# Latent attention: scores made in both orientations, stacks loaded 16 channels at a time, GpSimd merging the diagonal

## The chip, the cores and the metric

The kernel runs on one core of one Trainium2 chip. The metric is the device time of one launch in microseconds (us). A core has a matrix engine (TensorE, PE in the profile, with PEld for its weight loads), a vector engine (VectorE, DVE), an activation engine (ScalarE, ACT), a general engine (GpSimd, POOL) and a queue that mostly issues DMAs (SyncE, SP). SBUF is the on-chip memory of 128 partitions; PSUM, also 128 partitions, has 8 banks of 512 f32 columns and takes what PE writes.

## The reference, cut to what matters

A two-layer decoder on x of shape 2 x 1024 x 256. The change touches only the first block, a latent attention with 16 heads of 16 channels, on the layer-normalised x:

```python
q, k, v = x @ Wq, x @ Wk, x @ Wv
latent_kv = (k + v) @ W_down_kv             # 64 wide
k_rec, v_rec = latent_kv @ W_up_k, latent_kv @ W_up_v
scores = clip(einsum('bhqd,bhkd->bhqk', qh, kh) / 16, -1e4, 1e4)
decay  = exp(-0.0001 * abs(i - j))          # i query, j key
scores = clip(scores * decay, -1e4, 1e4)
attn   = softmax(scores); out = (attn @ vh) @ Wo
```

After it come a cross attention over 77 context tokens, a quantised feed-forward, a linear attention, a second cross attention and a mixture of experts. None of these is changed.

## The kernel before, in words

The program is a row of blocks; within a block each engine runs its own list in order, and semaphores order the engines against each other. Where one block ends, all engines wait until the last is done, DMAs included. The blocks that matter here are `normalise` (leaves the normalised x turned in `k.xt`), `latent_projections`, `latent_attention` and `project_out`.

`latent_projections` (L302) walks 4 groups of 512 tokens. For each group PE makes four pieces of 128 channels by 512 tokens (two of q, two of k, L350 and L357), the latent (L339) and the values (L364). Each piece is split into three bf16 parts whose sum is the f32 value: ACT rounds (L422), DVE subtracts (L383) and takes the largest magnitude (L385), ACT rounds the rest (L429), DVE makes the third part (L390). SP stores the three parts to DRAM (L445), 384 KB a piece, 16 pieces.

`latent_attention` (L451) runs over 16 heads in a loop, two batches in its body, 8 query tiles of 128 each: 256 steps. Before each head and batch SP loads a stack of 96 rows for q and for k (six bands of 16 channels, which are the products of parts that are kept), 12 DMAs of 32 KB (L537, L541). A step, in the order of the engines:

- PE makes the scores of one query tile against 1024 keys, two matmuls of 512 columns (L578), into two PSUM banks. Two steps are in flight.
- DVE multiplies them with the decay and takes the row maximum in one instruction, out to SBUF (L659).
- POOL negates the maximum (L563), ACT takes the exponential of 1024 columns with it as bias and sums the row (L706).
- Three steps later PE turns the probabilities in eight 128 x 128 transposes (L588) into two banks, ACT copies three of four such banks back to SBUF (L521), DVE the fourth (L519).
- PE sums the values: `mix_part` (L603), each matmul with 32 weight columns, four side by side into the four quarters of a bank, 128 moving columns each. A short copy, a transpose and a scaling (L695, L612, L640) end four query tiles.

When POOL has negated the last maximum it clears a DRAM buffer of 5 MB used much later (`clear_slots`, L116). That DMA belongs to the block too.

The cross attention block (L733 on) is not changed, but it has instructions of the kinds the change uses: exponentials read straight from PSUM (L1019), a value sum with 512 moving columns in four column quarters (L871), and a maximum split in three bf16 parts on POOL (L930 to L936).

Of the kernel before, what the change touches and what calls it, by code (L numbers as in the profile page):

```python
# [21 lines left out]
P = 128  # L22
# [279 lines left out]
def latent_projections(k, v_heads, q_scratch, k_scratch):  # L302
# [5 lines left out]
    qk_ready, part1_done, rest1_done, part2_done, part3_done = (  # L308
        k.sem("qk_ready"), k.sem("part1_done"), k.sem("rest1_done"), k.sem("part2_done"), k.sem("part3_done"))
    v_ready, v_done = k.sem("v_ready"), k.sem("v_done")  # L310
    bound_own, largest_ready, largest_turned = k.sem("bound_own"), k.sem("largest_ready"), k.sem("largest_turned")
    stored = [k.sem(f"stored{s}") for s in range(4)]
    scale = 1.0 / 16.0
    NP = NG * 2 * KD
    with ExitStack() as c, nc.Block() as block:
# [3 lines left out]
        parts = k.sb(c, "parts", [P, 4, 3, G], BF16)  # L319
        rest = k.sb(c, "rest", [P, 4, G])  # L320
        largest = k.sb(c, "largest", [P, NP])
# [5 lines left out]
        def _(pe):  # L327
# [14 lines left out]

            latent(0)
            for g in range(NG):
                rows = slice(g * G, (g + 1) * G)
                for m in range(KD):
                    n = 4 * g + m
                    wait(pe, rest1_done, n - 3)
# [5 lines left out]
                for m in range(KD):  # L354
                    n = 4 * g + 2 + m
                    wait(pe, rest1_done, n - 3)
# [4 lines left out]
                for j in range(TPG):  # L361
                    t = g * TPG + j
                    wait(pe, v_done, t - 1)
                    pe.matmul(k.ps[:, 5 + t % 2, 0:D], lat[:, t * P:(t + 1) * P], k.wuv[:, :],  # L364
                              start=True, stop=True).then_inc(v_ready, 1)
# [6 lines left out]
        def _(dve):  # L372
# [4 lines left out]
            for g in range(NG):  # L377
                for n in range(4 * g, 4 * g + 4):
                    s = n % 4
                    dve.wait_ge(part1_done, n + 1)  # L380
                    wait(dve, part2_done, n - 3)
                    wait(dve, part3_done, n - 3)
                    dve.scalar_tensor_tensor(out=rest[:, s, :], in0=k.ps[:, s, :], scalar=scale if s < 2 else 1.0,  # L383
                                             in1=parts[:, s, 0, :], op0=ALU.mult, op1=ALU.subtract).then_inc(rest1_done, 1)
                    own.did(dve.tensor_reduce(largest[:, n:n + 1], parts[:, s, 0, :], AX, ALU.max, apply_absolute_value=True))  # L385
                for n in range(4 * g, 4 * g + 4):
                    s = n % 4
                    dve.wait_ge(part2_done, n + 1)
                    dve.wait_ge(rest1_done, n + 1)
                    dve.tensor_tensor(parts[:, s, 2, :], rest[:, s, :], parts[:, s, 1, :],  # L390
                                      ALU.subtract).then_inc(part3_done, 1)


            own.wait()
            by_piece = largest[:, :].rearrange("p (g a m) -> p g a m", a=2, m=KD)
            for side in range(2):
                ins = dve.tensor_reduce(sides[:, side:side + 1], by_piece[:, :, side, :], mybir.AxisListType.XY, ALU.max)
                if side == 0:
                    own.did(ins)
                    own.wait()  # L400
            ins.then_inc(largest_ready, 1)
# [5 lines left out]
            own.did(dve.tensor_scalar(k.inside[:, :], bound[:, :], 0.9 * CLAMP / HD, None, ALU.is_lt))  # L407
            own.wait()

        @block.scalar  # L410
        def _(act):
# [3 lines left out]

            copy_latent(0)
            for g in range(NG):
                for n in range(4 * g, 4 * g + 4):
                    s = n % 4
                    act.wait_ge(qk_ready, n + 1)  # L420
                    wait(act, stored[s], 16 * g)
# [29 lines left out]
def latent_attention(k, v_heads, attn, decay, q_scratch, k_scratch):  # L451

    nc = k.nc
    k.next_block()
# [1709 lines left out]
```

## Time and profile before

| what | us |
|---|---|
| median of 3 runs | 1612.59 (1612.44 to 1614.67) |
| the profiled execution's own time | 1615.76 |
| its span in the trace | 1614.2 |
| latent projections, from their first work to the next block's | about 22.7 to 84.0 |
| latent attention, to the first work of the output projection | 84.0 to 622.2 |

PE is busy 83% of the span, DVE 57%, ACT 58%, POOL 12%. A row of groups gives line, engine and operation, names, shapes and count, then busy time and the mean duration of one, then idle time before. A timeline row gives start, length, engine, line, names and count. Instructions on one engine overlap at their ends, so the distance of two starts, not the length of one, is what an instruction costs in a stream.

### The profile page before, as it was taken

To read this page: it belongs to the slowest core of one execution; us is meant where nothing else is said; L and a number is where in the kernel's file an instruction comes from. 1 tells how busy PE (TensorE), PEld (TensorE's weight loads), DVE (VectorE), ACT (ScalarE), POOL (GpSimd) and SP (SyncE) were. 2 spreads that over 40 slices of the span, in tenths; PEclk is the share of its full clock that TensorE was granted. 3 is DMA by queue.
4 is the path that set the end of the run, shared out by engine and by line. 5 is a ranking of instruction groups with operands and counts; after the bars stand their busy time and mean duration, and the time that the engine had idled before them with its cause. 6 is when DMAs were issued, how large, how long until landed. Compare 5 with 4: busy or idle time off the path is not lost. (4 is left out here: it accounts for less than half of the span.)

```text
span 1614.2 us, 36474 instructions
## 1 busy us (share of the span) xinstructions
PE 1340.0 (83%) x12288; PEld 960.2 (59%) x12291; DVE 919.8 (57%) x2059; ACT 930.1 (58%) x1793; POOL 190.5 (12%) x546
## 2 busy tenths in 40 slices
PE   5879999999999995898365699889874489999992
PEld 2347777777777774544223464364354279999992
DVE  5558888888888873532788844563354223323233
ACT  2469999999999991355375377624631033333330
POOL 0001111111111110111200000031120701111110
PEclk9879999999999997899756899988995589999996
DMA  3311010010101013200000100033006211111115
GB/s 115 131 51 31 22 27 24 24 26 23 29 20 29 20 38 110 80 1 4 16 1 0 31 1 1 1 120 129 1 4 212 102 34 36 37 36 38 36 33 166
DMA packets 60025, 74.30 MB, mean 46 GB/s; under 512 B 13006, under 2 KB 47728, under 8 KB 59952
## 3 DMA queue, kind: packets, MB, share of 16 engines
q1 hardware_dynamic: 53168, 56.76, 11.9%
q0 software_dynamic: 4672, 14.50, 2.7%
q10 hardware_dynamic: 2112, 2.10, 0.4%
q8 instruction: 43, 0.70, 0.2%
q14 instruction: 30, 0.25, 0.0%
HBM read 50.43 MB, written 22.88 MB: 45 GB/s over the span
## 5 line engine op out<-in xcount | busy, mean ns | idle before, releaser
L659 DVE CUSTOM_DVE_ANT_0 probs_sb<-banks,decay_sb 128x1024 f32<-128x1024 f32 x256 | 308.2, 1221 | 43.6 <-PE banks L578 22.5
L706 ACT ACTIVATE probs_sb<-probs_sb,shift_sb 128x1024 f32<-128x1024 f32 x256 | 294.8, 1151 | 18.1 <-POOL shift_sb L563 16.4
L588 PEld LDWEIGHTS banks<-ident_sb,probs_sb 128*128 128x128 f32 x2048 | 238.3, 141 | 55.1 <-issue 22.9
L588 PE MATMUL banks<-ident_sb,probs_sb 128*128 128x128 f32 x2048 | 267.8, 274 | 0.9 <-ACT probs_t_sb L521 0.8
L521 ACT ACTIVATE probs_t_sb<-banks 128x512 f32<-128x512 f32 x384 | 214.7, 597 | 4.1 <-PE banks L588 2.3
L578 PE MATMUL banks<-k_stack_sb,q_stack_sb 96*128 96x512 bf16 x512 | 156.9, 389 | 14.0 <-DMA k_stack_sb<-k_parts 10.7
L603 PE MATMUL banks<-probs_t_sb,v_head_sb 128*32 128x128 f32 x4096 | 151.2, 277 | 0.7 <-ACT probs_t_sb L521 0.7
L1846 PEld LDWEIGHTS banks<-slots_xt_sb,tile_w_sb 128*128 128x128 f32 x1248 | 146.5, 193 | 1.9
L1846 PE MATMUL banks<-slots_xt_sb,tile_w_sb 128*128 128x128 f32 x1248 | 146.6, 276 | 0.0
L1858 PE MATMUL banks<-experts_w_sb,xt_sb 128*128 x624 | 141.2, 379 | 1.3 <-issue 1.3
L1892 ACT ACTIVATE slots_xt_sb<-banks 128x256 f32<-128x256 f32 x39 | 14.9, 383 | 213.8 <-PE banks L1832 213.8
L1858 PEld LDWEIGHTS banks<-experts_w_sb,xt_sb 128*128 128x128 f32 x624 | 115.5, 190 | 15.8 <-issue 1.7
L519 DVE COPY probs_t_sb<-banks 128x512 f32<-128x512 f32 x128 | 88.6, 692 | 57.7 <-PE banks L588 56.0
L603 PEld LDWEIGHTS banks<-probs_t_sb,v_head_sb 128*32 128x32 f32 x4096 | 100.3, 109 | 32.3 <-issue 31.4
L563 POOL TENSOR_TENSOR shift_sb<-peak_sb,minus_sb 128x1 f32<-128x1 f32 x256 | 48.5, 190 | 452.8 <-DVE peak_sb L659 452.8
L977 DVE TENSOR_REDUCE peak_sb<-banks 128x8 f32<-128x616 f32 x64 | 49.9, 798 | 87.8 <-PE banks L826 87.8
L1019 ACT ACTIVATE pt_sb<-banks,keyfill_sb 77x1024 f32<-77x1024 f32 x64 | 67.5, 1104 | 38.0 <-PE banks L857 37.1
L1902 ACT ACTIVATE xt_sb<-banks,tile_b_sb 128x128 f32<-128x128 f32 x312 | 84.7, 387 | 5.1 <-PE banks L1846 3.4
L1942 DVE COPY tile_w_sb<-experts_w_sb 128x2048 f32 x39 | 47.8, 1227 | 60.2 <-issue 28.0
L1927 DVE TENSOR_TENSOR is_best_sb<-slots_x_sb,tile_owned_sb 128x1 f32<-128x1 f32 x39 | 6.2, 159 | 122.2 <-DMA outputs_y<-slots_y_sb,output_row_sb 122.2
L253 POOL TENSOR_TENSOR x_sb<-x_sb,bb_sb 128x256 f32<-128x256 f32 x48 | 33.0, 732 | 337.2 <-DMA bb_sb<-in_L_attn_bo 276.7
L1881 POOL DMA_INDIRECT outputs_y<-slots_y_sb,output_row_sb x39 | 37.4, 959 | 258.7 <-DVE slots_y_sb L1955 154.0
(289 smaller groups left out, 1910.0 us busy)
## 6 DMA issues: line engine op xcount, KB each, us to landing
experts_w_sb<-in_L_ffn_W SPq DMA_DIRECT2D x16, 1024.0 KB, 11.9
q_stack_sb<-q_parts SPq DMA_DIRECT2D x192, 32.0 KB, 1.7
k_stack_sb<-k_parts SPq DMA_DIRECT2D x192, 32.0 KB, 1.8
slots_x<-zeros_sb POOLq DMA_DIRECT2D x1, 5031.0 KB, 22.6
slots_x_sb<-slots_x SPq DMA_DIRECT2D x39, 129.0 KB, 2.1
xt_sb<-outputs_y SPq DMA_DIRECT2D x8, 512.0 KB, 5.5
q_parts<-parts_sb SPq DMA_DIRECT2D x8, 384.0 KB, 3.0
k_parts<-parts_sb SPq DMA_DIRECT2D x8, 384.0 KB, 4.2
```

The source lines that it names most:

```text
L519: ins = eng.tensor_copy(dst, k.ps[:, 4 + half, :])
L521: ins = eng.activation(dst, k.ps[:, 4 + half, :], ACT.Copy)
L578: last = pe.matmul(k.ps[:, 2 * (s % 2) + half, :], qs[:, u, q * P:(q + 1) * P], ks[:, u, half * 512:(half + 1) * 512], start=True, stop=True)
L588: last = pe.transpose(k.ps[:, 4 + half, j * P:(j + 1) * P], pr[:, s % 4, (half * TPG + j) * P:(half * TPG + j + 1) * P], k.ident[:, :])
L603: last = pe.matmul(k.ps[32 * j:32 * j + 32, 6, 0:P], vh[:, u, kt, :], pt[:, j, gs % 2, kt, :], start=kt == 0, stop=kt == QT - 1)
L659: dve.tensor_tensor_reduce(out=pr[:, s % 4, :], in0=scores, in1=decay[:, off:off + S], scale=1.0, scalar=-3.0e38, op0=ALU.mult, op1=ALU.ma ...
L706: act.activation(pr[:, s % 4, :], pr[:, s % 4, :], ACT.Exp, bias=shift[:, s % 8:s % 8 + 1], accum_out=sums[:, (s // TPG) % 4, s % 4:s % 4 ...
L977: dve.tensor_reduce(peak[:, t % TPG, 2 * half:2 * half + 2, :], k.ps[:, bank:bank + 2, 0:SLOTS * C].rearrange("p r (s n) -> p r s n", n=C) ...
L1019: act.activation(pt[:, n % 2, 2 * half:2 * half + 2, :], k.ps[0:C, 2 * half:2 * half + 2, :], ACT.Exp, bias=key_fill[:, b:b + 1]).then_inc ...
L1846: last = pe.matmul(k.ps[:, 2 * u + f // HALF, (f % HALF) * P:(f % HALF + 1) * P], w1[:, u, kd, f * P:(f + 1) * P], xst[:, u, kd, :], start ...
L1858: last = pe.matmul(k.ps[:, 6, s * D:(s + 1) * D], ht[:, s, f, :], r.w2[:, bass.ds(e, 1), f, :].rearrange("p a n -> p (a n)"), start=f == 0 ...
L1902: ins = act.activation(ht[:, s, f, :], k.ps[:, 2 * s + f // HALF, (f % HALF) * P:(f % HALF + 1) * P], ACT.Gelu_apprx_tanh, bias=b1[:, s, f ...
```

## The change

`latent_projections` now makes two versions of every piece. Version 0 is multiplied by exp(-0.0001 i) for q and exp(+0.0001 j) for k, version 1 by the inverse, with a sign. The product of a version's q and k is then the score with its decay already in it, on one side of the diagonal. DVE multiplies and takes the maximum in one instruction (from PSUM), ACT rounds twice, DVE subtracts once and the third part is made by POOL. There are 32 pieces instead of 16, six buffers instead of four, and 32 stores of 384 KB. Two fade rows and two tables of the decay's width are loaded at the start of this block instead of one table before it. When the first batch's pieces are stored, SP also loads the first stacks.

`latent_attention` is written out without a loop, in 16 groups of four heads by four query tiles (512 queries). The four heads of a channel lie behind one another in DRAM, so that a load of 16 channels brings four heads: 256 KB for k, 128 KB for q. Per group:

- 16 query-major score tiles as before (1024 columns each, cut in two or three matmuls where the version changes), which now serve the maximum alone (`highest`: the same DVE instruction, its output unused). They run 22 tiles ahead of what follows.
- POOL splits the 16 x 2 maxima in three bf16 parts, PE turns them, ACT copies them, and one DMA writes them as rows 96 to 98 of the q stack. The k stack has -1 in those rows, so the key-major product comes out with the maximum taken off.
- Eight key tiles (steps): four key-major score matmuls of 512 queries, one a head, each followed by one exponential of 512 columns from PSUM to SBUF, through a ring of three banks. No probability is turned and no bank copied.
- On a tile that crosses the diagonal, every second step, a fifth unit makes 128 queries of the four heads in the other version. POOL keeps the later half of one and the earlier half of the other (`affine_select` twice) and adds them.
- Two steps later PE sums the values: four matmuls of 512 columns, side by side. The row sum comes from a column of ones in the values.
- Every group: four transposes, a reciprocal and a scaling.

```diff
-            pe.wait_ge(exp_done, n + 1)                       # turn: 8 transposes a step
-                        last = pe.transpose(k.ps[:, 4 + half, j * P:(j + 1) * P], ...
+            def select(g, i):
+                ...
+                pool.wait_ge(exp_done, unit_index(g, i, HEADS - 1) + 1)
+                pool.affine_select(later, later, [[0, HEADS], [1, P]], ALU.is_ge, 0.0, base=0,
+                                   channel_multiplier=-1).then_inc(selected, 1)
+                earlier = probs_d[:, s // 2 % 2, :, :]
+                pool.wait_ge(exp_done, unit_index(g, i, HEADS) + 1)
+                pool.affine_select(earlier, earlier, [[0, HEADS], [-1, P]], ALU.is_gt, 0.0, base=0,
+                                   channel_multiplier=1).then_inc(selected, 1)
+                pool.wait_ge(selected, 2 * (s // 2 + 1))
+                pool.tensor_tensor(later, later, earlier, ALU.add).then_inc(merged, 1)
```

The order on PE, and what it waits for:

```diff
+            pe.wait_ge(constants, 2)
+            for tile in range(TILES + LEAD):              # 22
+                scores(tile)
+                if tile == TILES + 1:
+                    turn_peaks(0)
+            for g in range(GROUPS):                       # 16
+                for i in range(QT):                       # 8
+                    if g * QT + i >= 2:
+                        sum_values(g * QT + i - 2)        # waits merged on odd i
+                    for x in range(2):
+                        for h in range(2 * x, 2 * x + 2):
+                            key_scores(g, i, h)           # waits for the bank three units back
+                        if x == 1 and i == TURN_STEP and g + 1 < GROUPS:
+                            turn_peaks(g + 1)
+                        if tile_at(g, i, x) < GROUPS * TILES:
+                            scores(tile_at(g, i, x))
+                    if on_diagonal(i):
+                        diagonal_scores(g, i)
+                    if i == 3 and g > 0:
+                        turn_mix(g - 1)
```

What POOL does at the start of the block, before PE may begin:

```diff
+            own.did(pool.memset(vh[:, :, :, :, :], 0.0))                                        # 128 x 2048 f32
+            own.wait()
+            pool.memset(stacks.k[ROWS:ROWS + PARTS, :, :, :, :], -1.0).then_inc(constants, 1)   # 3 x 16384 bf16
+            pool.wait_ge(constants, 1)
+            pool.tensor_copy(ident_b[:, :], k.ident[:, :]).then_inc(constants, 1)
```

In `latent_projections`:

```diff
+            def apply_fade(e):
+                ...
+                wait(dve, part3_done, e - 3)
+                dve.tensor_tensor_reduce(out=rest[:, e % 4, :], in0=k.ps[:, n % 4, :], in1=fade[:, side, half * G:(half + 1) * G], ...
+        @block.gpsimd
+            for e in range(NV):                           # 32
+                pool.wait_ge(part2_done, e + 1)
+                pool.wait_ge(rest1_done, e + 1)
+                pool.tensor_tensor(parts[:, e % SLOTS, 2, :], rest[:, e % 4, :], parts[:, e % SLOTS, 1, :],
+                                   ALU.subtract).then_inc(part3_done, 1)
```

`clear_slots` still comes last on POOL, after the last `select`.

## Rows read from the trace of the kernel before

**Rows 1.** Busy time by stretch: PE, PEld, DVE, ACT, POOL, then PE clock, DMA share, GB/s.

```profile
22.70:84.00 61.30, 48.26 (x106) 20.25 (x106) 31.60 (x55) 25.43 (x53) 0.00 (x0) 0.81 0.31 103
100.00:580.00 480.00, 476.15 (x6316) 352.36 (x6315) 388.70 (x724) 468.25 (x905) 53.56 (x272) 1.00 0.10 25
...
700.00:710.00 10.00, 8.94 (x87) 4.03 (x85) 3.03 (x5) 5.86 (x7) 1.67 (x8) 1.00 0.00 1
```

**Rows 2.** Groups by line, whole span.

```profile
L659 DVE CUSTOM_DVE_ANT_0 probs_sb<-banks,decay_sb 128x1024 f32<-128x1024 f32 x256 | 308.2, 1221 | 43.6 <-PE banks L578 22.5 <-issue 13.7 <-PE banks L588 4.4
L706 ACT ACTIVATE probs_sb<-probs_sb,shift_sb 128x1024 f32<-128x1024 f32 x256 | 294.8, 1151 | 18.1 <-POOL shift_sb L563 16.4
...
L521 ACT ACTIVATE probs_t_sb<-banks 128x512 f32<-128x512 f32 x384 | 214.7, 597 | 4.1 <-PE banks L588 2.3
```

**Rows 3.** Timeline, a steady step of latent attention: PE's three kinds of work, ACT's copies.

```profile
301.34 0.65 PE L603 MATMUL banks<-probs_t_sb,v_head_sb 128*32 128x128 f32 x16
...
301.92 0.60 PE L578 MATMUL banks<-k_stack_sb,q_stack_sb 96*128 96x512 bf16 x2
...
302.36 1.04 PE L588 MATMUL banks<-ident_sb,probs_sb 128*128 128x128 f32 x8
...
303.00 1.09 ACT L521 ACTIVATE probs_t_sb<-banks 128x512 f32<-128x512 f32 x2
```

**Rows 4.** Timeline, the cross attention: value sum with 512 columns, exponentials from PSUM.

```profile
702.55 0.38 PE L857 MATMUL banks<-peakt_sb,minus_one_sb 12*77 12x512 bf16 x2
702.78 2.11 ACT L1019 ACTIVATE pt_sb<-banks,keyfill_sb 77x1024 f32<-77x1024 f32 x2 [0.96 <-PE banks L857]
...
702.86 1.06 PE L871 MATMUL banks<-pt_sb,va_sb 77*32 77x512 f32 x8
...
703.86 0.30 PE L821 MATMUL banks<-hidden_sb,fillb_sb 3*128 3x308 bf16 x2
```

**Rows 5.** Groups of POOL, by shape.

```profile
L253 POOL TENSOR_TENSOR x_sb<-x_sb,bb_sb 128x256 f32<-128x256 f32 x48 | 33.0, 732 | 337.2 <-DMA bb_sb<-in_L_attn_bo 276.7 <-DMA bb_sb<-in_L_xattn_bo 60.5
...
L559 POOL COPY v_head_sb<-v_heads_sb 128x128 f32 x28 | 8.1, 289 | 3.2 <-issue 3.1
...
L936 POOL TENSOR_TENSOR peakparts_sb<-peakrest_sb,peakparts_sb 128x16 bf16<-128x16 f32 x32 | 7.1, 220 | 2.6
...
L930 POOL CAST peakparts_sb<-peak_sb 128x16 bf16<-128x16 f32 x32 | 6.3, 196 | 120.3 <-issue 63.7 <-DVE peak_sb L977 56.7
L923 POOL MEMSET peakparts_sb<- 128x1024 bf16 x2 | 2.4, 1178 | 70.8 <-POOLq L160 70.8
```

**Rows 6.** Timeline, the start of latent attention.

```profile
83.99 2.67 SPq L537 DMA_DIRECT2D q_stack_sb<-q_parts  x6
...
85.33 0.52 POOL L548 MEMSET v_head_sb<- 128x512 f32 x1 [84.88 <-issue]
...
90.91 1.89 PE L578 MATMUL banks<-k_stack_sb,q_stack_sb 96*128 96x512 bf16 x4 [10.71 <-DMA k_stack_sb<-k_parts]
...
92.11 1.23 DVE L659 CUSTOM_DVE_ANT_0 probs_sb<-banks,decay_sb 128x1024 f32<-128x1024 f32 x1 [11.11 <-PE banks L578]
...
94.58 1.23 DVE L659 CUSTOM_DVE_ANT_0 probs_sb<-banks,decay_sb 128x1024 f32<-128x1024 f32 x1
```

**Rows 7.** Timeline, the end of latent attention and the next block's first work.

```profile
599.24 2.22 POOL L116 DMA_DIRECT2D slots_x<-zeros_sb  x1 [0.32 <-POOL zeros_sb L114]
...
622.23 3.65 PE L261 MATMUL banks<-ident_sb,attn_sb 128*128 128x128 f32 x16 [14.82 <-PEq L475]
```

**Rows 8.** Timeline, latent projections: ACT's and DVE's splitting, PE's matmuls.

```profile
29.35 3.70 PE L350 MATMUL banks<-xt_sb,L_attn_Wq_sb 128*128 128x512 f32 x8
...
52.05 2.17 ACT L429 ACTIVATE parts_sb<-rest_sb 128x512 bf16<-128x512 f32 x4
52.70 2.50 DVE L390 TENSOR_TENSOR parts_sb<-rest_sb,parts_sb 128x512 bf16<-128x512 f32 x4 [0.62 <-ACT parts_sb L429]
...
55.60 5.40 PE L350 MATMUL banks<-xt_sb,L_attn_Wq_sb 128*128 128x512 f32 x8
```

**Rows 9.** DMA issues: size, and median us from issue to landing.

```profile
k_parts<-parts_sb SPq DMA_DIRECT2D x8, 384.0 KB, 4.2
```

More of the change, by code:

```diff
@@ L360, in _ @@
                     latent(g + 1)
[L361 to L365, printed above, removed]
+            for m in range(KD):
+                values(NG - 1, m)
             pe.wait_ge(largest_ready, 1)
@@ L376, in _ @@
             dve.tensor_copy(wkv[:, :, :], k.ps[:, 7, 0:KD * L].rearrange("p (m n) -> p m n", m=KD)).then_inc(wkv_done, 1)
[L377 to L391, printed above, removed]
@@ L438, in _ @@
         def _(sp):
-            for n in range(NP):
+            for v in range(2):
+                sp.dma_start(fade[:, v, :], fade_in[v].partition_broadcast(P)).then_inc(fade_arrived, 16)
+            later.start(sp)
+            for e in range(NV):
+                n, version = divmod(e, 2)
                 g, s = divmod(n, 4)
@@ new lines, in _, with load_stacks @@
+                if 20 <= e < 26:
+                    load_stacks(sp, stacks, 0, e - 20)
+            for x in range(SLOTS):
+                sp.wait_ge(stored[x], 16 * len(range(x, NV, SLOTS)))
+            later.wait(sp)
+class Stacks:
+    pass
+HEADS = 4
+def load_stacks(eng, stacks, g, piece):
+    n, half = divmod(g, 2)
+    b, first = divmod(n * HEADS, H)
+    rows = slice(b * D + first * HD, b * D + (first + HEADS) * HD)
+    q_part, k_part = [(0, 0), (0, 1), (0, 2), (1, 0), (1, 1), (2, 0)][piece]
+    dst = slice(piece * HD, (piece + 1) * HD)
+    if half == 0:
+        eng.dma_start(stacks.k[dst, n % 2, :, :, :].rearrange("p v h n -> p v (h n)"),
+                      stacks.k_scratch[:, k_part, rows, :].rearrange("v (p h) n -> p v (h n)", h=HEADS)
+                      ).then_inc(stacks.arrived[g % 3], 16)
+    eng.dma_start(stacks.q[dst, g % 3, :, :, :].rearrange("p v h n -> p v (h n)"),
+                  stacks.q_scratch[:, q_part, half, rows, :].rearrange("v (p h) n -> p v (h n)", h=HEADS)
+                  ).then_inc(stacks.arrived[g % 3], 16)
@@ new lines, in _ @@
+            own.wait()
+            stage_values(0)
+            split_peaks(0)
+            for g in range(GROUPS):
+                for i in range(QT):
+                    if on_diagonal(i):
+                        select(g, i)
+                    if i == 3 and g % 2 == 0 and g + 2 < GROUPS:
+                        stage_values(g // 2 + 1)
+                    if i == TURN_STEP - 1 and g + 1 < GROUPS:
+                        split_peaks(g + 1)
+            clear_slots(k, pool, zeros_set)
@@ L711, in _, with exponential @@
-            steps(act, step)
+            def exponential(g, i, h):
+                u, s = unit_index(g, i, h), g * QT + i
+                act.wait_ge(key_scored, u + 1)
+                act.wait_ge(released, u + 1)
+                if h == 0:
+                    wait(act, summed, s - 2)
+                if h < HEADS:
+                    out = probs_of(s)[:, h, :]
+                else:
+                    wait(act, merged, s // 2 - 1)
+                    out = probs_d[:, s // 2 % 2, :, :].rearrange("p h n -> p (h n)")
+                act.activation(out, k.ps[:, bank_of((exp_done, u + 1)), :], ACT.Exp).then_inc(exp_done, 1)
```

636 lines of the change are left out of this document (387 added, 249 removed).

## The prediction

> **What bounds the kernel now.** I read the busy time by stretch first, then the groups by line, then the timeline of one steady step, and last the timelines at the block's two ends. The stretch table shows that between 100 and 580 us PE is busy 476 of 480 us and ACT 468, at a granted clock of 1.00 [rows 1]: latent attention keeps two engines full at once, 538 us long (84.0 to 622.2) [rows 6, 7]. ACT has 3.75 instructions a step (one exponential with its sum read out, 1.5 copies, a quarter of a short copy), and 905 of them in 480 us make 1.99 us a step. The groups say what fills ACT: 256 exponentials of 1.15 us and 384 copies of 0.60 [rows 2]. The timeline says what fills PE [rows 3]: 0.44 us for a tile's two score matmuls (301.92 to 302.36), 0.88 for eight transposes (302.36 to the next work at 303.24), 0.58 for 16 value instructions (301.34 to 301.92), together 1.90 of the 1.99. So a change pays only if it takes work from PE and from ACT together. This one does: transposes and copies go. What has to be found is what is late next.
>
> **The main loop, part by part.** A pair of steps (one with the diagonal, one without) is the unit; there are 64.
>
> PE. A key unit and half a query tile are 512 bf16 columns each, 0.22 us [rows 3]. A value sum has its own row in the cross attention: eight instructions of 512 columns in four quarters take 1.00 us to the next work (702.86 to 703.86), and 0.09 us pass before them (0.22 after 702.55, to 702.86) [rows 4]: 1.1. The diagonal unit is four matmuls of 128 columns, between 0.22 (by columns) and 0.44 (by the transposes' 0.11); I take 0.25. The extra cuts where a version changes add no columns; at nothing, at most 0.05 us each. A step without the diagonal is 1.1 + 4 x 0.22 + 2 x 0.44 = 2.86, one with it 3.11, a pair 5.97.
>
> ACT. Copies of 512 columns from PSUM start 0.49 us apart (two in 1.09, one 0.60) [rows 2, 3]; two exponentials of 1024 from PSUM take 2.11 together [rows 4], so 0.53 for 512. At 0.5 a pair of nine is 4.5. DVE: four maxima at 1.2 [rows 2], 4.8. Neither bounds. The old row maximum stays whole on DVE, hidden under PE.
>
> The merge on POOL is the new wait, and PE stands behind it: the value sum of a diagonal tile waits for it, and behind that wait in PE's list stand the next key units, so ACT, and the next query tiles, so DVE. Its pieces: the add, 512 columns with two inputs. POOL's 256 columns take 0.732 and 16 take 0.220, so 2.13 ns a column and 1.28 us for 512 [rows 5]. The selection has no row. From below it is a copy with one input: 0.196 for 16, 0.289 for 128, so 0.83 ns a column and 0.61 us. From above it is a two-input operation, 1.28. One input in, one out, the index formed beside it: it is nearest the copy, and I take 0.7. Counted from PE's issue of the diagonal unit: the last ordinary exponential is done at 0.7, the diagonal one at 1.15 (0.4 to the end of the matmuls, 0.6 of exponential, a hand-over). Selection to 1.4, selection to 2.15, add to 3.45, PE goes on at 3.55. PE would be there after the diagonal unit and one plain step, 0.25 + 2.86 = 3.11. So it waits 0.44 each time, and a pair is 2.86 + 3.55 = 6.41 us. In general a pair is 2.86 + max(3.11, 2.15 + two selections): beyond a selection of 0.48 each 0.1 us of it costs 12.8 us of the kernel. 64 x 6.41 = 410 us. The eleven last steps have no query tiles but hang on the same chain (6.2 a pair), so they stay in the count.
>
> The Trainium skill speaks here (GPSIMD Engine Reference, 3.1 and 4.1): plain elementwise work belongs on VectorE, GpSimd being about half as fast with two inputs. The trace agrees: 512 columns cost DVE 0.62 (four in 2.50) [rows 8]. The same page puts the best software loop at 769 ns for 512 elements; by that the selection would be 0.77 and the loop 9 us longer.
>
> Per group: four transposes (0.44), and the turn of the maxima, which waits for DVE's last tile of the group (1.2) and four short POOL operations (about 0.28 each with hand-over, from 0.2 each [rows 5]); PE arrives some 2.5 us after that tile, so about 0.4 is left. 16 x 0.8 = 13 us. Loop 423 us.
>
> **The start.** Before, the block began at 84.0 and the first scores came at 90.9, held by twelve stack loads [rows 6]. Those are now behind the projections, but PE waits for POOL's constants instead. POOL begins at 1.3 us. 2048 f32 columns of zeros are at most four times 0.52, 2.1 us [rows 6]. The -1 rows are only three partitions, but 16384 bf16 columns each: 1024 took 1.178 us [rows 5], so with 0.1 of it fixed 17.3 us; bounds 8 (if two bf16 go as one f32) and 18.8. With the identity's copy the first scores come at 21, 14 us later than before. Then 22 tiles run alone before the first key unit. The first two maxima took 2.47 us (92.11 to 94.58) with PE still slow [rows 6]: 1.2 to the first, 20 x 1.235, 0.9 for the last: 27 us with ACT idle, where before the first exponential followed the first scores by 3. The maxima's way (split, turn, copy, one DMA) fits in the last six tiles.
>
> **The end.** After the last diagonal unit 3.4 us of merge, then `clear_slots`. Its DMA was issued at 599.24 and the next block began at 622.23, 23.0 later, 23.3 with the memset: the block waits for that, not for the last value sum [rows 7]. Before, POOL was free a few us ahead of the end, as now.
>
> **The projections.** 32 pieces through three engines: DVE 0.6 (half of 1.2) + 0.62 [rows 2, 8]; ACT twice 0.54 (four in 2.17) [rows 8] and 0.25 of other copies, 1.35; POOL 1.28 + 0.1 = 1.38 [rows 5]. At 1.4 to 1.45 POOL needs 46 us after a first piece at about 35, then a last store of 4.2 [rows 9]: the block ends near 87 instead of 84. Six buffers at 1.4 cover a store's 4.2. PE needs 20 passes of 512 columns a group: 0.43 each at 2.4 GHz, 8.6 us against 11.5 available, but 17 at 1.2 GHz; both paces are in the trace (eight in 3.70 and in 5.40 [rows 8], clock 0.81 on the stretch [rows 1]). I take 3 us longer, between -6 (DVE's pace) and +20 (PE slow throughout).
>
> **The sum.** 87 + 21 + 27 + 423 + 3.4 + 23.3 = 585 where the trace has 622: 37 us less. The profiled execution took 1615.8, the median of the runs is 3.2 lower; so 1578 for the profiled one, 1575 as a median.
>
> **Rivals.**
>
> 1. GpSimd's selections go like two-input work, 1.28 us. Then the pair is 2.86 + 4.71 = 7.57, the loop 74 us longer, 1649 us: slower than before. The turning point is a selection of 0.99 us (37 us over 128 selections). For it: no row shows the operation, it must form and compare an index per element, and the skill's own best loop already lies above the copy. Against it: only one operand is read. 22%.
>
> 2. PE alone bounds: the merge hides and the pair is 5.97, 28 us less, and the constants come cheaper (8 instead of 17), 9 us less: 1538. For it: a selection at 0.61 leaves only 0.26 us of wait. Against it: the add alone is 1.28. 15%.
>
> 3. The projections, with twice the pieces, run at PE's slow clock: +17 more than I count, 1592. For it: the 0.81 of the stretch. Against it: PE's pauses get shorter there. 7%.
>
> 4. PE's clock falls to 1.2 GHz in the main loop because PE stands still at every merge and in front of a ring of three banks. A pair then is some 11.5 us; over half the loop +160 us, 1735. Against it the cross attention: PE busy 8.94 of 10 us with a pause in every unit and a clock of 1.00 [rows 1]; my loop has 5.97 of 6.41. 4%. The Trainium skill names this (TensorE: Matmul & The Clock Gate, "A second HAM failure mode"): cycling through PSUM banks with small pauses can make the clock swing. No stretch here shows it.
>
> That the clipping path would be taken, because the bound for it is tighter, I leave out: it is one constant of 0.81 and the fade's 11% on each side, and the trace shows the short path (the maximum reads the banks directly [rows 6]).
>
> **How the numbers follow.** My case has 52%, with 1550 to 1605 as its own range. A measurement of this kernel tells 0.2% (3.2 us) from no change. Faster: nearly all of my case, 2 and 3, and rival 1's lower edge: 0.70. Same: 0.03. Slower: the most of rival 1, and 4: 0.27. The range takes in rival 2 and most of rival 1: 1535 to 1640.
>
> **What would show it.** First scores about 21 us into the block and a POOL memset of about 17 us; first exponential from the ring 27 later; value sums of diagonal tiles waiting about 0.4 us for POOL's add, 64 times; no wait on DVE or ACT of note; the selection's mean, which decides most; a clock of 1.00 in the loop; the next block 23 us after the last add. Wrong if PE's pair without waits is above 6.3 (small matmuls or the switch to quarters dearer), or if ACT's ring, and not POOL, holds PE.

## The result and the profile after

| | before | changed |
|---|---|---|
| median, us (lowest to highest, runs) | 1612.51 (1611.95 to 1614.67, 4) | 1633.20 (1631.49 to 1635.07, 4) |
| the profiled execution, us | 1615.76 | 1631.49 |
| its span, us | 1614.2 | 1629.4 |

The ratio is 1.0126, 95% interval 1.0108 to 1.0144: 1.3% slower. The forecast was 1575, faster; 1633 lies inside its range, near the upper end, and none of the four rivals is what happened.

The next block's first work comes at 637.03, where the sum gave 585 and the trace of before has 622.23 [rows 7]. First the busy time by stretch of the changed kernel, with the columns of [rows 1]: the projections, the main loop, and seven slices of the loop around the start of a group.

```profile
21.80:108.70 86.90, 51.08 (x106) 19.52 (x106) 48.85 (x103) 44.37 (x84) 46.68 (x32) 0.75 0.74 207
153.00:612.00 459.00, 403.87 (x2688) 156.28 (x2685) 290.11 (x502) 306.69 (x604) 175.09 (x256) 0.96 0.36 45
384.00:388.00 4.00, 3.70 (x24) 1.19 (x21) 3.17 (x6) 2.34 (x6) 2.25 (x3) 1.00 1.10 150
388.00:392.00 4.00, 3.85 (x28) 1.44 (x27) 2.38 (x4) 3.66 (x8) 1.38 (x3) 1.00 1.03 113
392.00:396.00 4.00, 3.52 (x26) 1.49 (x26) 2.90 (x5) 2.67 (x6) 1.11 (x1) 1.00 0.98 107
396.00:400.00 4.00, 4.00 (x31) 1.66 (x33) 3.27 (x7) 2.85 (x7) 3.04 (x4) 1.00 1.05 117
400.00:404.00 4.00, 1.40 (x12) 0.31 (x4) 1.55 (x4) 1.53 (x3) 0.91 (x4) 1.00 0.98 107
404.00:408.00 4.00, 1.64 (x7) 0.99 (x8) 0.43 (x1) 0.14 (x1) 0.00 (x0) 0.50 0.02 2
408.00:412.00 4.00, 4.00 (x23) 1.61 (x22) 2.04 (x4) 2.12 (x5) 2.21 (x3) 0.65 0.04 8
```

The DMA engines are fully busy for 20 us and move only 107 to 150 GB/s. PE stands still from 401.4 until 406.4, and its granted clock falls to 0.50. The timeline names the wait (start, length, engine, line, names, count, idle before and its end):

```profile
400.79 0.61 PE L653 MATMUL banks<-q_stack_sb,k_stack_sb 99*128 99x256 bf16 x4
...
406.37 1.03 PE L646 MATMUL banks<-k_stack_sb,q_stack_sb 96*128 96x128 bf16 x3 [4.96 <-DMA q_stack_sb<-q_parts]
...
409.57 1.65 PE L690 MATMUL banks<-probs_sb,v_head_sb 128*32 128x512 f32 x8
...
412.03 0.60 PE L653 MATMUL banks<-q_stack_sb,k_stack_sb 99*128 99x512 bf16 x2
```

The waits of PE over the loop (us in total, times, longest), and below them the DMA issues by size (KB each, median us from issue to landing):

```profile
PE banks L646 <- DMA q_stack_sb<-q_parts: 29.8, 6, 5.8
PE banks L690 <- POOL xt_sb L776: 9.3, 23, 0.9
PE banks L690 <- POOL probs_sb L776: 5.5, 11, 0.9
PE banks L698 <- ACT xt_sb L915: 3.2, 6, 0.5
```

```profile
k_stack_sb<-k_parts SPq DMA_DIRECT2D x48, 256.0 KB, 12.0
q_stack_sb<-q_parts SPq DMA_DIRECT2D x96, 128.0 KB, 5.4
```

The merge, which the forecast had made the new bound, takes as long as forecast. One diagonal tile on POOL and PE:

```profile
265.27 0.64 POOL L769 TENSOR_SCALAR_AFFINE_SELECT xt_sb<-xt_sb 128x512 f32<-128x512 f32 x1 [3.71 <-ACT xt_sb L915]
...
265.86 0.64 POOL L773 TENSOR_SCALAR_AFFINE_SELECT probs_d_sb<-probs_d_sb 128x512 f32<-128x512 f32 x1
...
266.58 1.27 POOL L776 TENSOR_TENSOR xt_sb<-xt_sb,probs_d_sb 128x512 f32<-128x512 f32 x1
...
267.99 1.06 PE L690 MATMUL banks<-xt_sb,v_head_sb 128*32 128x512 f32 x8 [0.30 <-POOL xt_sb L776]
```

The start of the block, beside [rows 6], and its end, beside [rows 7]:

```profile
108.69 2.65 SPq L519 DMA_DIRECT2D q_stack_sb<-q_parts  x6
110.00 1.80 POOL L737 MEMSET v_head_sb<- 128x2048 f32 x1 [7.19 <-issue]
...
111.86 13.75 POOL L739 MEMSET k_stack_sb<- 3x16384 bf16 x1
...
125.68 0.29 POOL L741 CAST ident_b_sb<-ident_sb 128x128 bf16<-128x128 f32 x1
...
126.02 1.89 PE L646 MATMUL banks<-k_stack_sb,q_stack_sb 96*128 96x128 bf16 x6 [21.77 <-POOL ident_b_sb L741]
...
153.04 1.06 PE L653 MATMUL banks<-q_stack_sb,k_stack_sb 99*128 99x512 bf16 x2
...
615.95 2.23 POOL L116 DMA_DIRECT2D slots_x<-zeros_sb  x1 [0.32 <-POOL zeros_sb L114]
...
637.03 3.22 PE L261 MATMUL banks<-ident_sb,attn_sb 128*128 128x128 f32 x14 [17.79 <-PEq L589]
```

And the projections, whose end is 108.69 where 87 was forecast. PE's wait for a bank of the values at the start of a group, its first q piece of that group, DVE's wait for it, and two subtractions, one alone and one beside POOL:

```profile
41.78 1.22 PE L354 MATMUL banks<-wuv_sb,lat_sb 64*128 64x256 f32 x2 [5.38 <-ACT v_heads_sb L457]
...
44.48 3.78 PE L366 MATMUL banks<-xt_sb,L_attn_Wq_sb 128*128 128x512 f32 x4
...
48.44 0.69 DVE L399 CUSTOM_DVE_ANT_0 rest_sb<-banks,fade_sb 128x512 f32<-128x512 f32 x1 [6.09 <-PE banks L366]
...
50.27 0.69 DVE L405 TENSOR_TENSOR rest_sb<-rest_sb,parts_sb 128x512 f32<-128x512 f32 x1
51.48 1.04 DVE L405 TENSOR_TENSOR rest_sb<-rest_sb,parts_sb 128x512 f32<-128x512 f32 x1
```

The values of the group before (L354) stand in PE's list between this group's pieces (L366). They go through two banks that ACT copies one by one between its other work, so PE waits 30.2 us for ACT's L457 in this stretch, and the pieces are late.

POOL's third parts, the first and the last of the stretch (there are 32):

```profile
30.93 13.54 POOL L436 TENSOR_TENSOR parts_sb<-rest_sb,parts_sb 128x512 bf16<-128x512 f32 x9 [30.41 <-ACT parts_sb L452]
...
100.55 2.26 POOL L436 TENSOR_TENSOR parts_sb<-rest_sb,parts_sb 128x512 bf16<-128x512 f32 x2 [3.44 <-ACT parts_sb L452]
```

They begin at 30.93 and end at 102.81, 71.9 us later, where the forecast had 46 after a start at 35.

| step | forecast | measured | difference |
|---|---|---|---|
| latent attention begins | 87 | 108.69 | +21.7 |
| to the first scores | 21 | 17.3 | -3.7 |
| lead until the first key scores | 27 | 27.0 | 0 |
| loop until the last key scores (612.0) | 423 | 459 | +36 |
| last merge and clearing, to the next block's first work | 26.7 | 25.0 | -1.7 |

The differences make 52.3; 637.03 less the sum's 584.7 is the same. The median is 58 us above the forecast. The rest is mostly in how the profiled execution lies to the median: the forecast took 3.2 us off for it, and this time the profiled execution was 1.7 below the median.

### The profile page after: what moved, and what is told of

The parts are those of the page before. It is cut to its first block and busy times, and to the rows that moved or that the text cites. A ratio compares the mean times of both kernels' runs of the same rounds, so it can differ in the third digit from the quotient of the medians.

```text
span 1629.4 us, 25126 instructions
## 1 busy us (share of the span) xinstructions
PE 1261.3 (77%) x8338; PEld 744.7 (46%) x8339; DVE 839.3 (52%) x1883; ACT 761.0 (47%) x1473; POOL 375.0 (23%) x556
## 5 line engine op out<-in xcount | busy, mean ns | idle before, releaser
L816 DVE CUSTOM_DVE_ANT_0 faded_scores_sb<-banks,inner_sb 128x1024 f32<-128x1024 f32 x256 | 304.5, 1222 | 159.6 <-PE banks L646 158.4
L915 ACT ACTIVATE xt_sb<-banks 128x512 f32<-128x512 f32 x344 | 179.6, 602 | 102.4 <-PE banks L653 102.4
L646 PE MATMUL banks<-k_stack_sb,q_stack_sb 96*128 96x512 bf16 (+3 forms) x704 | 169.5, 348 | 55.9 <-DMA q_stack_sb<-q_parts 29.8
L653 PE MATMUL banks<-q_stack_sb,k_stack_sb 99*128 99x128 bf16 (+3 forms) x960 | 185.9, 304 | 5.8 <-ACT xt_sb L915 2.6
L653 PEld LDWEIGHTS banks<-q_stack_sb,k_stack_sb 99*128 99x128 bf16 x960 | 74.8, 100 | 164.7 <-ACT xt_sb L915 66.0
L646 PEld LDWEIGHTS banks<-k_stack_sb,q_stack_sb 96*128 96x128 bf16 x704 | 66.8, 103 | 120.8 <-DMA q_stack_sb<-q_parts 31.5
L915 ACT ACTIVATE probs_sb<-banks 128x512 f32<-128x512 f32 x168 | 87.6, 603 | 47.0 <-PE banks L653 47.0
L690 PE MATMUL banks<-xt_sb,v_head_sb 128*32 128x512 f32 x688 | 94.8, 623 | 11.7 <-POOL xt_sb L776 11.6
L769 POOL TENSOR_SCALAR_AFFINE_SELECT xt_sb<-xt_sb 128x512 f32<-128x512 f32 x43 | 27.3, 636 | 167.8 <-ACT xt_sb L915 167.8
L436 POOL TENSOR_TENSOR parts_sb<-rest_sb,parts_sb 128x512 bf16<-128x512 f32 x32 | 46.7, 1489 | 55.6 <-ACT parts_sb L452 55.6
```

What stands on the lines that cost most here:

```text
L436: pool.tensor_tensor(parts[:, e % SLOTS, 2, :], rest[:, e % 4, :], parts[:, e % SLOTS, 1, :], ALU.subtract).then_inc(part3_done, 1)
L646: last = pe.matmul(k.ps[:, 2 * (tile % 2) + half, lo - half * G:hi - half * G], stacks.q[0:ROWS, g % 3, version, h, j * P:(j + 1) * P], st ...
L653: return pe.matmul(k.ps[:, bank, at:at + hi - lo], stacks.k[0:ROWS + PARTS, g // 2 % 2, version, h, kt * P:(kt + 1) * P], stacks.q[0:ROWS ...
L690: last = pe.matmul(k.ps[VW * h:VW * (h + 1), PV_BANK, :], vh[:, n % 2, h, kt, :], probs_of(s)[:, h, :], start=i == 0, stop=i == QT - 1, sk ...
L816: dve.tensor_tensor_reduce(out=junk[:, tile % 2, :], in0=tile_scores(tile), in1=inner[:, window(tile)], scale=1.0, scalar=-3.0e38, op0=ALU ...
L915: act.activation(out, k.ps[:, bank_of((exp_done, u + 1)), :], ACT.Exp).then_inc(exp_done, 1)
```

## The experiments

The theory after this comparison: (1) a load into 16 adjacent partitions reaches only a small part of the rate that the DMA engines have, a set of twelve takes 20 us, and PE needs it some 18 us after its first issue; (2) the projections are held by PE's order; (3) the memset of the -1 rows is paid in full. Each edit below is of the changed kernel unless it says otherwise.

### e1_rows: the 16 channels into every sixth partition of 96

The order of rows in a stack is free as long as q and k agree.

```diff
-    dst = slice(piece * HD, (piece + 1) * HD)
+    dst = slice(piece, 6 * HD, 6)
```

> The changed kernel, with one edit: a load's 16 channels go to every sixth of the 96 partitions instead of 16 adjacent ones. Same loads, bytes and order. Theory A (a load into 16 adjacent partitions is what is slow: 2.36 MB in about 20 us): the set lands in under 9 us, PE's six waits for the stacks (29.8 us) go, and so do ACT's waits for the stores behind the first loads in the projections (8.4 us): 1595 us, between 1588 and 1603. Rival B (the bytes, the DRAM side or the size of the pieces are what is slow): landing times and the time stay, 1633 us.

Measured: 1590.25 (1589.0 to 1592.7), 0.9868 of before (0.9851 to 0.9884). The landings, and the loop at the same work:

```profile
k_stack_sb<-k_parts SPq DMA_DIRECT2D x48, 256.0 KB, 4.7
q_stack_sb<-q_parts SPq DMA_DIRECT2D x96, 128.0 KB, 3.5
```

```profile
149.38:568.60 419.22, 390.52 (x2687) 150.97 (x2685) 290.11 (x502) 305.92 (x604) 175.45 (x256) 0.99 0.20 49
```

One line of layout is worth 43 us. The same bytes land 2.6 times as fast for k; PE's wait for DMA is gone, the loop takes 419 us instead of 459 (29.8 of the 40 were the wait itself, the rest lies with the lower clock behind it: PE is busy 390.5 us instead of 403.9 for the same matmuls, and the value sums after the pause took 1.65 instead of 1.06), and attention begins 3.7 us earlier. ACT's waits for the stores, 8.4 us in the projections, are gone.

### e2_order: the second half of the values behind the group's pieces

```diff
-                    if g > 0:
-                        values(g - 1, m)
+                    if g > 0 and m == 0:
+                        values(g - 1, 0)
...
                 if g + 1 < NG:
                     latent(g + 1)
+                if g > 0:
+                    values(g - 1, 1)
```

> The changed kernel, with one edit in the projections: PE makes the second half of the last group's values after the group's four pieces, not between the two q pieces. Theory A (PE is tied to ACT's copies there, and DVE starves 5.6 to 6.1 us at three group starts): the three gaps go, 16 us less, 1617 us (1610 to 1623). Rival B (GpSimd's third parts and the stores behind them set the pace, so the gaps are caught up anyway): 1628 to 1633 us.

Measured: 1622.57 (1620.51 to 1624.18). Attention begins at 97.77 instead of 108.69, DVE and POOL now run through two groups without a gap:

```profile
40.00:60.00 20.00, 16.68 (x38) 5.93 (x36) 20.00 (x40) 17.35 (x35) 20.00 (x13) 0.91 0.75 251
```

POOL is busy 20.00 of 20 us with 13 pieces, a piece in some 1.55 us. POOL's third parts, first and last:

```profile
32.20 40.63 POOL L438 TENSOR_TENSOR parts_sb<-rest_sb,parts_sb 128x512 bf16<-128x512 f32 x26 [31.68 <-ACT parts_sb L454]
...
89.65 2.26 POOL L438 TENSOR_TENSOR parts_sb<-rest_sb,parts_sb 128x512 bf16<-128x512 f32 x2 [2.70 <-ACT parts_sb L454]
```

They take 59.7 us, 12.2 less than in the changed kernel. PE's waits for DMA in the loop stay (29.0). The order was worth 10.9 us in the trace, 10.6 in the median, inside the stated range, but 16 were expected. DVE's waits for PE's q pieces do fall by 16 us (21.8 to 5.7), and part is given back: ACT's waits for the stores rise from 8.4 to 12.4 us.

### e3_consts: half of the -1 rows in `normalise`, half at the start of the projections

```diff
+        @block.gpsimd                                   # in normalise
+            pool.memset(constants, -1.0)                # k stack, buffer 0
...
+            pool.memset(stacks.k[6 * HD:6 * HD + 3, 1, :, :, :], -1.0).then_inc(rows_set, 1)   # projections
+            pool.wait_ge(rows_set, 1)
             for e in range(NV):
...
-            pool.memset(stacks.k[ROWS:ROWS + PARTS, :, :, :, :], -1.0).then_inc(constants, 1)
```

> The changed kernel, with one edit: GpSimd writes the -1 rows earlier, one half during the normalisation and one at the start of the projections, where it is idle. Theory A (PE's first scores wait for that memset of 13.75 us alone): first scores 3.6 us into the block instead of 17.3, 1619 us (1616 to 1622). Rival B (something else holds the first scores or the first key units, such as the loads of the second and third group, issued at the same time, in front of the DMA that brings the maxima): 1626 to 1633 us.

Measured: 1626.71 (1623.98 to 1631.58): 6.5 us less where 14 were expected. That is a time of rival B, but not for B's reason: the first scores do come 3.7 us into the block. The block itself begins at 119.62 instead of 108.69 (the profiled execution is the slowest of the four, 4.9 us above their median). The delay begins in the normalisation. One short instruction of DVE there, in the changed kernel:

```profile
12.36 0.17 DVE L189 TENSOR_SCALAR var_sb<-mv_sb 128x16 f32<-128x16 f32 x1
```

and here, beside POOL's first memset, with the second memset and POOL's first parts below:

```profile
11.52 6.92 POOL L176 MEMSET k_stack_sb<- 3x8192 bf16 x1 [10.99 <-POOLq L131]
...
12.40 6.07 DVE L194 TENSOR_SCALAR var_sb<-mv_sb 128x16 f32<-128x16 f32 x1
...
28.03 6.92 POOL L438 MEMSET k_stack_sb<- 3x8192 bf16 x1 [9.59 <-POOLq L160]
...
38.35 12.37 POOL L443 TENSOR_TENSOR parts_sb<-rest_sb,parts_sb 128x512 bf16<-128x512 f32 x8 [3.40 <-ACT parts_sb L459]
```

DVE's instruction ends at 18.47, as POOL's memset does (18.44), and takes 6.07 us instead of 0.17. All that follows is 5.7 to 5.9 us later. The half in the projections held nothing: POOL is done with it at 34.95 and then waits 3.40 us for ACT. Of the 10.9 us by which the block begins later, POOL's first part accounts for 7.4 (30.93 to 38.35). Of those, 5.9 are this wait; most of the other 1.5 lies in PE's first matmuls and comes without the edit too (POOL's first part at 32.20 in e2_order). The remaining 3.5 lie between the projections' groups and stay open. POOL was idle in the normalisation, but DVE beside it was not.

### e4_three: the three edits together

> The three edits together. If each hits a separate wait: 1633 - 38 - 16 - 14 = 1565 us (1555 to 1578), faster than the kernel before by 3%. Rival: they overlap in the projections, where the stores wait behind the first loads: then 1578 to 1590 us.

Measured: 1564.96 (1564.78 to 1565.67), 0.9709 of before (0.9693 to 0.9725). The time is the one expected, but partly by luck: the expectation added 38, 16 and 14, the single edits gave 43.0, 10.6 and 6.5, together 60, and the three at once gave 68. Some 6 of the other 8 us can be seen in the projections. POOL's memset and its third parts, first and last:

```profile
28.82 6.92 POOL L440 MEMSET k_stack_sb<- 3x8192 bf16 x1 [10.47 <-POOLq L160]
40.56 42.12 POOL L445 TENSOR_TENSOR parts_sb<-rest_sb,parts_sb 128x512 bf16<-128x512 f32 x27 [4.82 <-ACT parts_sb L461]
...
89.73 2.27 POOL L445 TENSOR_TENSOR parts_sb<-rest_sb,parts_sb 128x512 bf16<-128x512 f32 x2 [0.81 <-ACT parts_sb L461]
```

The third parts take 51.4 us, 8.3 less than in e2_order (the spread rows alone, in e1_rows, took 2.5 off this stretch, 71.9 to 69.4), and ACT's waits for the stores fall by the same 8.3 (12.4 to 4.1). So once PE's order is put right, the stores behind the narrow first loads are what is late, and the spread rows are worth more than they were alone. The loop takes 418.9 us. The forecast's picture (1575, loop 423) was that of a kernel whose loads and projections do not get in its way.

### e6_consts: the channels, the order, and all -1 rows in `normalise`, as 8192 f32 words

Two bf16 of -1 are written as one f32.

```diff
+            minus_ones = stacks.k[6 * HD:6 * HD + 3, :, :, :, :].rearrange("p a v h n -> p (a v h n)").bitcast(F32)
+            normalise(k, loads, constants=minus_ones)
```

> The changed kernel with spread rows and the new order of the values, and the -1 rows written as 8192 f32 words in the normalisation's block instead of two bf16 halves (e4_three had one half at the start of the projections, where it held up GpSimd). If the memset costs per element, it takes about 6.9 us, ends before the normalisation does, and the projections are 4 to 6 us shorter than with e4_three: 1560 us (1556 to 1563). Rival (it costs per byte, 13.75 us, and ends after the normalisation): 1563 to 1567 us.

Measured: 1566.53 (1563.82 to 1569.45), 0.9704 of before, no gain on e4_three (0.9709), and a time of the rival. The memset of 8192 f32 takes 6.92 us, the same as one of 8192 bf16 above: the cost goes by elements, so packing halves it, as the theory had it. What was wrong is the premise that the half in the projections held POOL up: in e4_three POOL is done with it at 35.74 and waits 4.82 us for ACT (rows above). The memset that delays others is the one in the normalisation, and this edit keeps it: DVE's short instruction takes 6.07 us here too, and in every run below that has this memset. No run moves it out of DVE's way, so the fastest version still contains this delay; what its removal is worth was not measured.

### e7_clear: e6_consts with `clear_slots` after the ninth group

```diff
+                    if g == 8 and i == QT - 1:
+                        clear_slots(k, pool, zeros_set)
-            clear_slots(k, pool, zeros_set)
```

> As e6_consts, and the 5 MB DRAM buffer is cleared in the middle of latent attention (after group 8) instead of after GpSimd's last merge. The block's end no longer waits for that DMA (21.1 us from its issue to the next block's first work in e4_three, of which about 4 lie beside the last value sums): 16 to 18 us less, 1543 us (1540 to 1547). Rival (the DMA delays stack loads, or its descriptors hold GpSimd's merges): part of it is given back, 1548 to 1555 us.

Measured: 1551.44 (1549.22 to 1554.76), 15 us less than e6_consts where 16 to 18 were expected. The time falls into the rival's range, but because the expectation started from 1560 and e6_consts took 1566.5, not for the rival's reason: 5 MB moved in the middle of the loop cost it nothing (417.8 us, 418.9 in e4_three). The wait between the last value sum and the next block is now short:

```profile
547.75 1.07 PE L697 MATMUL banks<-xt_sb,v_head_sb 128*32 128x512 f32 x8 [2.31 <-POOL xt_sb L781]
...
554.16 2.15 PE L266 MATMUL banks<-ident_sb,attn_sb 128*128 128x128 f32 x9 [3.53 <-PEq L596]
```

### e8_pairs: every second partition of a band of 32

Between adjacent and spread over 96, to see whether it is the number of partitions spanned.

```diff
-    dst = slice(piece * HD, (piece + 1) * HD)
+    dst = slice(piece // 2 * 32 + piece % 2, piece // 2 * 32 + 32, 2)
```

> The changed kernel with one edit, half a dose of e1_rows: a load's 16 channels go to every second of 32 partitions, so that two loads share a band of 32. If the price is set by how many groups of adjacent partitions a load reaches, a set that took 20 us on 16 adjacent partitions lands in 10 to 11, before PE asks for it (16 us), and the time is near that of e1_rows: 1592 us (1588 to 1598). Rival (any step between partitions does it, or only the full width does): landing times as e1_rows, 5 us, or as the changed kernel, 12 us and 1633.

Measured: 1589.65 (1585.19 to 1593.12), the same as e1_rows. Landings lie between those of the changed kernel and of e1_rows, near the latter:

```profile
k_stack_sb<-k_parts SPq DMA_DIRECT2D x48, 256.0 KB, 5.3
q_stack_sb<-q_parts SPq DMA_DIRECT2D x96, 128.0 KB, 3.7
```

Doubling the span is enough to bring the set in before PE asks for it; more span brings the kernel nothing.

### e9_before_rows: the kernel before, its 32 KB loads spread over 96 partitions

```diff
-                                    sp.dma_start(stack[row + x * HD:row + (x + 1) * HD, u, :],
+                                    sp.dma_start(stack[row // HD + x:96:6, u, :],
```

> The kernel before, with the same edit as e1_rows in its own loads (16 channels of 2 KB to every sixth partition). There a load is 32 KB and SP issues one each 0.45 us, so at the 118 GB/s of 16 adjacent partitions it takes 0.28 us, less than its issue. Theory: no change, 1612 us (1609 to 1614), first scores about 90.9 us as before. Rival (the narrow target costs there too): 3 to 8 us less.

Measured: 1615.19 (1613.63 to 1617.58, 10 runs), ratio 1.0006 (0.9994 to 1.0018): no change, against the 1614.31 that the kernel before took beside it. The first scores come at 93.14, 2.2 us later than before and not at 90.9 as expected, because the spread loads take SP longer to issue (six in 3.73 us instead of 2.67). The fault is not in the layout of before: its loads are off the path. The change made them eight times (k) and four times (q) as large and left the layout as it was.

### e5_twice: e4_three with PE summing a diagonal tile's two halves itself

This undoes the change's own idea: POOL only selects, PE adds the second half with four matmuls of 128 columns.

```diff
-                pool.tensor_tensor(later, later, earlier, ALU.add).then_inc(merged, 1)
...
+                if on_diagonal(i):
+                    lo = block_of(g, i) * P
+                    for h in range(HEADS):
+                        last = pe.matmul(k.ps[VW * h:VW * (h + 1), PV_BANK, lo:lo + P], vh[:, n % 2, h, kt, :],
+                                         probs_d[:, s // 2 % 2, h, :], start=False, stop=i == QT - 1, ...)
```

> e4_three, with GpSimd's add left out: PE sums a diagonal tile's two halves itself, with four more value matmuls of 128 columns. The merge chain loses 1.27 us, so PE's waits for it (17 us in 35 places) go; the added matmuls cost 0.21 us of columns and some set-up, 64 times 0.25 to 0.35 is 16 to 22 us. Theory (PE sets the pace, and the wait for the merge is about as dear as the second sum): 1565 us, within 5. Rival A (the merge is the bound): 1550 or less. Rival B (the second sum is dearer than its columns): 1575 or more.

Measured: 1558.19 (1556.3 to 1560.42), some 7 us less than e4_three and below the 1560 to 1570 that was expected; neither rival's time was reached. The loops of e4_three and of e5_twice, one line each:

```profile
127.87:546.80 418.93, 390.23 (x2686) 150.81 (x2685) 290.10 (x502) 305.72 (x604) 175.47 (x256) 0.99 0.20 49
```

```profile
126.90:537.70 410.80, 400.17 (x3187) 165.46 (x3184) 290.05 (x502) 305.13 (x603) 95.14 (x193) 1.00 0.21 50
```

PE is busy 9.9 us more and waits less: its waits for POOL were 14.9 us in e4_three, and 1.0 for the halves here. The loop is 8.1 us shorter. The add saved PE less than waiting for it cost.

### e10_before_clear: the kernel before, `clear_slots` after its first head

```diff
-            bodies(pool, body)
-            clear_slots(k, pool, zeros_set)
+            bodies(pool, body, lambda: clear_slots(k, pool, zeros_set))
```

> The kernel before, with the 5 MB buffer cleared after the first head instead of at the end, the edit of e7_clear. The next block's first work came 14.8 us after the last one of latent attention: 12 to 15 us less, 1599 us (1597 to 1602). So the fair comparison of the repaired change with the kernel before is e7_clear against this one.

Measured: 1601.73 (1600.04 to 1603.93), 0.993 of before (0.9903 to 0.9956), as expected. This gain is not the change's; versions with the early clearing are to be held against 1601.7.

### e11_best: e7_clear with e5_twice's edit

> The changed kernel with everything that the runs so far found: channels spread over 96 partitions, values after the pieces, the -1 rows written as f32 words in normalise, clear_slots after group 8, and PE summing a diagonal tile's two halves itself. Theory: the last edit took 6.8 us off the kernel with the first three (1565.0 to 1558.2), and clear_slots is out of the way, so the end of the loop counts fully: 1551.4 - 7 = 1544 us (1540 to 1548). Rival A, the gain was the removed merges in front of the loop's end (the last merge stands on the path to clear_slots there) and not in the loop: 1551 (1549 to 1554). Rival B, with GpSimd's merge gone the loop becomes the exact sum of PE's work and the diagonal's extra matmuls cost what the waits did: 1551 too, but with PE's waits for GpSimd at 0 to 1 us and PE's busy time 16 us higher.

Measured: 1541.05 (1538.62 to 1544.0), 0.956 of before (0.9535 to 0.9585), as expected: the fastest version, 92 us less than the changed kernel. The loop takes 410.6 us and PE is busy 399.8 of it. Against e10_before_clear it is 0.962 (1541.05 by 1601.73, from two sets of runs, so without an interval).

## Why the prediction was wrong

**The step that failed first: the loads were never priced in the loop.** The prediction counted the twelve stack loads at the start ("are now behind the projections") and nowhere else. In the kernel before, the loads were 32 KB each and off the path (e9_before_rows). After the change a set of twelve is 2.36 MB (six of 256 KB, six of 128). The DMA engines need 20 us for it (the slices from 384 to 404, at 107 to 150 GB/s), and 2.4 more pass until PE goes on. PE asks for the set 18 us after its first issue (383.4 to 401.4) and goes on after 23.0. Six such waits, 29.8 us, and the clock behind each make 40 of the loop's 459 us; the rest of the loop came 4 under its forecast, and so the +36. Shown by e1_rows and e8_pairs, which change nothing but the partitions.

The Trainium skill has the rule that would have priced it (SBUF — State Buffer, "Door 1: The DMA port swizzle"): a DMA's rate goes by how many of 16 SBUF ports its partitions reach, groups of four neighbours share one, and all 16 together give about 435 GB/s. Sixteen adjacent partitions reach four ports, an estimate of 109 GB/s from that page; the measured slices have 107 to 117. By the page every second of 32 reaches eight; in e8_pairs the k load's landing went from 12.0 us to 5.3. No run separates the ports from other ways in which the partitions could matter; that the partitions are the cause is shown.

**The projections, 24.7 us longer than before where 3 were forecast.** The bounds were -6 to +20, from the engines' paces and PE's clock, so the result lies outside them. The forecast compared each engine's pace with its work and never walked PE's list. The stretch from POOL's first third part to the end of its last divides the error: 71.9 us in the changed kernel, 59.7 with the order alone (e2_order), 51.4 with the spread loads as well (e4_three; its third edit falls outside this stretch), 46 in the forecast. So 12.2 us are PE's order, 8.3 the first stack loads among the last stores, and 5.4 POOL's own term: a part costs 1.56 us in the stream (27 in 42.12), not 1.38 to 1.45. POOL began 4.1 earlier than the 35 assumed. Together that is the 21.7 of the table. The division depends on the order of the edits: the spread loads alone shorten this stretch by 2.5 only (e1_rows).

PE's clock in this stretch was 0.75, so the condition of rival 3 held in part. It is not what made the stretch long: in e2_order it was 0.91 between 40 and 60 us, where PE no longer waits at a group's start, but 0.76 over the whole stretch, and the stretch was still 10.9 us shorter. The prediction took its two paces of PE from rows of eight in 3.70 and in 5.40 us; the second is a mixture (granted clock 0.68 in it), not the slow pace alone.

**The constants, -3.7.** The memset took 13.75 us, not 17.3: 0.83 ns an element (8192 take 6.92, 16384 take 13.75), with the 0.1 us of fixed cost that was assumed. The row of 1024 elements in 1.178 us, from which the 17.3 came [rows 5], lies above this line, and no run shows why. The other memset in view, 512 elements in 0.52 us [rows 6], lies on it and would have given 13.5.

**What was right.** The lead (27.0 us). The selection, the term with most at stake: 0.636 us by its group, 0.64 in the rows above, against 0.7 forecast and rival 1's 1.28. The add: 1.27 against 1.28. The loop without the loads: 419 against 423, and that is partly luck. In it the waits for the merge were 14.9 us in 34 places, not 28 in 64; the waits behind ACT's exponentials were 11 us where the sum had 6, at the turn of the maxima; PE's own work was 393 us where it had 389. PE's own pair was (419.2 less 26 of waits) / 64 = 6.1 us with the per-group work in it, against 5.97 without. That rules out rival 1, and rival 2 in its strong form. Rival 4, a slow clock in the loop, came in a small way that was not named: not from small pauses at banks or merges, where the granted clock stayed 0.99 (e1_rows), but after pauses of 5 us (0.96 over the loop). The end was right too, but stood in the sum as given: e7_clear and e10_before_clear show that 15 and 12 us of it can be had.

## What to carry to other kernels

When a change alters the size or the count of a transfer, price it again everywhere it occurs: bytes by the rate of its own partitions, against the time until its reader asks, not only where it was on the path before. Here a DMA share of 1 with some 110 GB/s marked the transfers into few partitions; when a trace shows the like, try spreading the rows over the partitions if their order is free. And before summing engine paces, walk the list of the engine that feeds the others and look for an item in it that waits for a slower engine's small work. When work is moved to where its engine is idle, look at the engines beside it too, and measure edits together as well as singly: here three gave 68 us where their single gains add up to 60.

## What the runs showed of the hardware that was not expected

- A POOL memset can hold a DVE instruction until it ends. DVE's 128 x 16 TENSOR_SCALAR takes 0.17 us alone and 6.07 beside a memset of 6.92 us, in all six runs that have this memset in the normalisation (e3_consts, e4_three, e5_twice, e6_consts, e7_clear, e11_best). Not every instruction is held: in e3_consts DVE's BN aggregate, already running when the memset started, took its usual 1.17 us, and the copy from PSUM beside the second memset its usual 0.29.
- A POOL memset costs by elements: 8192 take 6.92 us as bf16 and as f32.
- POOL's subtraction and DVE's slow each other when they run together. In the changed kernel DVE's L405, with two inputs from SBUF, takes 0.69 us alone and 1.03 to 1.04 beside POOL (rows above); POOL's L436 goes between 1.15 and 1.6. DVE's L399, with one input from PSUM, stays at 0.68. The answer on POOL's line (ns: shortest, median, longest; first and last start):

```profile
L436 POOL TENSOR_TENSOR parts_sb<-rest_sb,parts_sb x32: 1146/1598/1607, 30.9 to 101.7; 128x512 bf16<-128x512 f32 x32
```

  The Trainium skill says this (SBUF — State Buffer, "SBUF: two separate sides"): a DVE instruction with two SBUF inputs and a GpSimd one that reads SBUF exclude each other. The lengthening by some 0.35 and 0.45 us agrees in kind; it is less than a full wait for the other.
- The profile page's mean for that group, 1489 ns, hides two kinds of instructions; the forecast's 1.38 us lies between them.
- After a pause of 5 us PE's granted clock was 0.50 (404 to 408), and the 4 us after it still had 0.65.
- Spreading partitions costs issue time on SP: six loads take 3.74 us (95.22 in e7_clear) instead of 2.65 (108.69 above).
